# One edge product for four tiles, in both edge layers of a graph network on one core

## The reference, cut to what matters

```
def _egnn_conv(x, src, dst, edge_attr, W_msg, W_edge, W_root, b):
    msg = x[src] @ W_msg + edge_attr @ W_edge
    agg = jax.ops.segment_max(msg, dst, num_segments=x.shape[0])
    agg = jnp.where(jnp.isneginf(agg), 0.0, agg)
    return agg + x @ W_root + b
c1 = jax.nn.leaky_relu(_egnn_conv(X, src, dst, edge_attr, W1_msg, W1_edge, W1_root, b1))
c2 = jax.nn.leaky_relu(_egnn_conv(c1, src, dst, edge_attr, W2_msg, W2_edge, W2_root, b2))
x = _layernorm(x + c2)
```

## Time and profile before

| what | value |
|---|---|
| runs | 5271.81 us median of 3 (5270.69 to 5279.11) |
| profiled execution | span 5177.2 us; the page gives no other time of it |
| layer a, about 1787 to 2493 us | TensorE 449, VectorE 340, ScalarE 123, GpSimd 377 us busy in 700 |
| layer b, about 2495 to 3190 us | TensorE 351, VectorE 462, ScalarE 258, GpSimd 377 us busy in 700 |
| edge products | 782 passes in each of the two layers |

### The profile page before, as it was taken

The page is one execution under the profiler, slowest core; times in us unless marked ns, Lnnn a source line. Parts: engine busy times, 40 slices in busy tenths (PEclk is TensorE's granted clock), DMA queues, the critical chain, the costliest instruction groups (busy, mean ns, idle before and its releaser), DMA issues. The chain is left out here.

```text
span 5177.2 us, 44582 instructions
## 1 busy us (share of the span) xinstructions
PE 2118.5 (41%) x9550; PEld 1632.7 (32%) x9550; DVE 2725.0 (53%) x10673; ACT 2076.4 (40%) x4598; POOL 2694.2 (52%) x2760
## 2 busy tenths in 40 slices
PE   5111584554545556766555553677671000000000
PEld 2000241144545446655333332567671000000000
DVE  8300695655555544545466676666674343434344
ACT  9100691044444411111233333455564443544444
POOL 6677004144444355555455554555554656566564
PEclk9655895567776765666555555565565555555555
DMA  1211004833333344444354454344442222222221
GB/s 54 44 39 36 5 1 121 224 100 100 102 98 106 104 129 156 152 154 153 113 157 151 151 160 130 129 149 141 138 140 67 64 62 64 64 61 66 58 70 41
DMA packets 361464, 524.87 MB, mean 101 GB/s; under 512 B 221626, under 2 KB 230607, under 8 KB 360938
## 3 DMA queue, kind: packets, MB, share of 16 engines
q1 hardware_dynamic: 267050, 366.82, 21.4%
q0 software_dynamic: 94144, 155.21, 12.9%
HBM read 230.29 MB, written 291.54 MB: 101 GB/s over the span
## 5 line engine op out<-in xcount | busy, mean ns | idle before, releaser
L1929 POOL DMA_INDIRECT out<-O,nidx x392 | 385.9, 984 | 374.3 <-ACT O L202 255.1
L1296 POOL DMA_INDIRECT l1a_G<-t,src x391 | 378.3, 967 | 319.8 <-issue 288.4
L1615 POOL DMA_INDIRECT l_G<-t,src x391 | 385.8, 987 | 304.2 <-issue 273.2
L637 POOL DMA_INDIRECT O<-x_pad,nidx x344 | 343.2, 998 | 367.7 <-PE en_psB L836 263.3
L1296 POOL DMA_INDIRECT l1b_G<-t,src x391 | 376.3, 962 | 301.1 <-issue 277.1
L2150 PE MATMUL l_psR<-l_diag,l_ones 128*128 128x128 f32 x2 | 0.8, 502 | 1241.7 <-DVE l_diag L2004 1241.7
L967 POOL DMA_INDIRECT l_G<-xs,src x327 | 312.5, 956 | 349.8 <-DVE l_G L996 229.8
L1914 POOL DMA_INDIRECT l_G<-t,src x391 | 375.8, 961 | 168.5 <-issue 118.9
L2150 PEld LDWEIGHTS l_psR<-l_diag,l_ones 128*128 128x128 f32 x2 | 0.5, 312 | 1241.8 <-DVE l_diag L2004 1241.8
L1494 PE MATMUL l1a_psP<-l1a_w,l1a_xT 97*128 97x192 f32 x784 | 250.0, 506 | 230.5 <-ACT l1a_xT L1411 157.4
L1473 PE MATMUL l1b_psE<-l1b_we,l1b_edge 32*128 32x96 f32 x782 | 197.6, 430 | 305.1 <-DMA l1b_edge<-edge_k 220.1
(11 more groups left out here) (347 smaller groups left out, 6757.0 us busy)
## 6 DMA issues: line engine op xcount, KB each, us to landing
h<-l_G SPq DMA_DIRECT2D x96, 392.0 KB, 2.3
t<-l1b_t_out SPq DMA_DIRECT2D x48, 768.0 KB
h<-l_G SPq DMA_DIRECT2D x48, 768.0 KB
xs<-en_y SPq DMA_DIRECT2D x48, 392.0 KB
t<-l_t_out SPq DMA_DIRECT2D x48, 392.0 KB
l_H<-t SPq DMA_DIRECT2D x48, 392.0 KB
en_y<-x_pad SPq DMA_DIRECT2D x48, 384.0 KB
t<-l_tr_out SPq DMA_DIRECT2D x48, 384.0 KB
```

The lines of the kernel that those rows point to most:

```text
L637: pool.indirect_dma_start(k.O[:, at, :], None, x, bass.IndirectOffsetOnAxis(k.nidx[:, at:at + 1], 0))\
L1296: pool.indirect_dma_start(tile(c)[:, q, :], None, table, bass.IndirectOffsetOnAxis(k.src[:, at:at + 1], 0))\
L1615: pool.indirect_dma_start(tile(c)[:, q, :], None, table, bass.IndirectOffsetOnAxis(k.src[:, at:at + 1], 0))\
L1929: pool.indirect_dma_start(out, bass.IndirectOffsetOnAxis(k.nidx[:, at:at + 1], 0), k.O[:, at, :], None, bounds_check=NP - 1, oob_is_err=Fa ...
```

## The change

The edge features of four tiles are stacked on the 128 partitions (tile i on partitions 32i to 32i+31), and the weight becomes a block-diagonal matrix of 128 by 384 with four copies of the 32 by 96 weight. One product then gives four tiles at once: the 96 columns of tile i come only from the partitions of tile i, since the other blocks are zero. The chunks of two and one tile take the columns that belong to their tiles. The features are laid out accordingly by the host, each half chunk as one block of 128 rows with 128 values. VectorE clears the weight first, and SyncE waits for that and loads the weight four times into the diagonal.

```
-        we = sb("we", [DE, D])
+        we = sb("we", [PACK * DE, PACK * D])          # PACK = Q // 2 = 4
-        edge = sb("edge", [DE, 2, Q // 2 * 128])
+        edge = sb("edge", [PACK * DE, 2, 128])
+        blank = sem("blank")
...
-            sp.dma_start(we[:, :], We).then_inc(weights, 16)
+            sp.wait_ge(blank, 1)
+            for i in range(PACK):
+                sp.dma_start(we[i * DE:(i + 1) * DE, i * D:(i + 1) * D], We).then_inc(weights, 16)
...
-                    sp.dma_start(edge[:, h, :], edge_k[c][:, h * 512:(h + 1) * 512]).then_inc(edge_in[h], 16)
+                    sp.dma_start(edge[:, h, :], edge_k[c, h]).then_inc(edge_in[h], 16)
...
+            dve.memset(we[:, :], 0.0).then_inc(blank, 1)
...
-            pe.wait_ge(weights, 64 if first else 16)
+            pe.wait_ge(weights, 16 * PACK + 48 if first else 16 * PACK)
...
-                    for i in range(n):
-                        part = edge[:, at // 4, (at % 4 + i) * 128:(at % 4 + i + 1) * 128]
-                        last = pe.matmul(V(c)[:, a + i, :], part, we[:, :],
-                                         start=first, stop=True, skip_group_check=not first)
-                    last.then_inc(edged, 1)
+                    mine = we[:, at % PACK * D:(at % PACK + n) * D].rearrange("p (q d) -> p q d", q=n)
+                    pe.matmul(V(c)[:, a:a + n, :], edge[:, at // PACK, :], mine,
+                              start=first, stop=True, skip_group_check=not first).then_inc(edged, 1)
...
-    by_tile = lambda a: whole(a.reshape(128, K, DE)).reshape(128, NCH, Q, -1).transpose(1, 3, 2, 0).reshape(NCH, -1, Q * 128)
+    by_tile = lambda a: whole(a.reshape(128, K, DE)).reshape(128, NCH, 2, Q // 2 * DE).transpose(1, 2, 3, 0)
```

More of the change, by code:

```diff
@@ L1172, in layer1 @@
     HELD = 3
+    PACK = Q // 2
     ctx = ExitStack()
```

## The result

The changed kernel takes 5212.47 us (median of 6 runs, 5201.7 to 5230.79) against 5271.25 us of the kernel before (6 runs, 5244.86 to 5286.93): ratio 0.9887, 95% interval 0.9854 to 0.992. A second series gave 5215.31 against 5264.3 us, ratio 0.993 (0.9892 to 0.9967). So the gain is some 37 to 59 us where 7 were forecast.

The account below looks back on a forecast made before the run. No engine was full: TensorE's loop bound part of layer a, standstills until GpSimd's gathers ended bound the rest and layer b. Terms 0 - 7 + 0 + 0 = -7 us took 5272 to 5265 us; range 5232 to 5290.

Parts of the forecast that it names:

- What of it lies on the path: Step asking where saved edge-product time on TensorE shortens layers a and b: 7 us in a, 0 in b.
- In layer b none: Layer b: edge products end 1.0 us ahead of VectorE, nothing waits for TensorE, so the gain is 0.
- 12 x 0.6 = 7 us: Layer a: half of VectorE's 23 waits for edge products each gain 0.6 us; bounds 0 and 18 us.
- The 12 even steps: Layer a: chunks assumed to run at the pace set by TensorE's loop, 12.84 us each, gaining 0.6 us each.
- no even steps near 12.1 us: Layer a: the forecast's sign was that chunks paced by TensorE's loop would shorten from 12.84 to near 12.1 us.
- more nameless waits: Layer a, VectorE's first addition: unnamed waits, 190.0 us before, should stay about as long; more or fewer meant wrong.
- the pause: Both layers: engines begin nothing although work is ready, until GpSimd's gathers are through; GpSimd stands 7.6 us per two chunks.
- The price of a product: Edge products: half a chunk takes 1.58 us instead of 1.94 in b; a chunk saves 0.6 us in a.
- Transfers and the start of a layer: Smaller edge packets, weight clearing and four weight loads: both terms 0; uncovered, the start costs at most 4 us in all.
- Rival 4: Layer b: small packets land edge features late, lengthening about half of 49 steps; +24 us, 5296 us, chance 0.06.
- rival 5: Layer a: TensorE works less, its clock stays lower and edge products take longer; about 5276 us, chance 0.07.
- Rivals 2 and 3: Layer a: the pace set by TensorE's loop spreads, 5230 us, chance 0.17; or is lost, 5284 us, chance 0.13.

Follow-up runs that it names:

- 512 columns: Changed kernel with each edge product streaming 512 columns instead of 384, the added ones zeros; 5215.73 us, ratio 0.9929 to the kernel before.
- layout only: Changed kernel's stacked features, block-diagonal weight and loads, but again one product per tile (782 passes); 5261.98 us, ratio 1.0034 to the kernel before.
- tiny6: Changed kernel with six small extra products ahead of each edge product (1366 passes a layer); 5283.69 us, ratio 1.0079 to the kernel before.
- tiny: Changed kernel with three small extra products ahead of each edge product (782 passes a layer); 5261.31 us, ratio 1.0031 to the kernel before.

## Why the prediction failed

**The step that failed** is "What of it lies on the path": "In layer b none" and, in a, 12 x 0.6 = 7 us. Both terms price the time of TensorE and ask who waits for it. In b indeed nobody does, and 31 us of added TensorE time cost nothing (512 columns). But the change takes 584 passes of TensorE from each layer, and the number of passes has a price of its own that isn't in the sum. Pooled over the profiles:

| | 782 passes | 198 passes | difference |
|---|---|---|---|
| layer a | 706.5 (707.8, 691.1, 714.8, 712.0, 706.8) | 680.2 (694.1, 671.0, 673.1, 682.7) | -26 us |
| layer b | 711.5 (700.1, 710.6, 714.0, 715.8, 717.2) | 689.8 (688.6, 691.3, 688.1, 691.2) | -22 us |

In b the two sets don't overlap; in a they do by one profile each, 691.1 against 694.1. The terms were 7 and 0 and measured 26 and 22: 48 us by the profiles, 37 to 59 by the two timed series. On the average between these two numbers that is 45 ns a pass in a and 37 ns in b; the twice as many small products, which left b at 711.1 us, show that it isn't a fixed price.

The 12 even steps of the 7 us weren't there either. By the places where GpSimd stood for over 1.5 us, 7 of the chunks of a in before are single steps, of 11.5 to 16.4 us each, and none in after, where all chunks behind the start go in pairs. So what a gained isn't what the term counted, and of the prediction's own signs two came out against it: no even steps near 12.1 us, and more nameless waits.

**The prediction named this and gave it no chance.** Its last paragraph says that if the pause "depends on how many instructions TensorE runs, both layers move by tens of microseconds". That is what happened. It had the evidence for a mechanism that doesn't go by waits on TensorE: 190 us of nameless waits in a, 4.59 us of idleness ahead of an instruction that needed only its own engine's results. A mechanism that takes 6 to 7 us out of every 27 deserved to be a rival with a price, even a rough one. That ScalarE's instructions count as well was not seen.

How the number acts shows in b. In before, VectorE is often held up well ahead of the last gathers too. Of before, the timeline of VectorE:

```profile
2824.53 1.92 DVE L1355 SCALAR_TENSOR_TENSOR l1b_R<-l1b_G,lastok,l1b_R 128x96 f32<-128x96 f32 x8
2828.26 0.97 DVE L1365 SCALAR_TENSOR_TENSOR l1b_psL<-l1b_R 128x768 f32<-128x768 f32 x1 [1.80 <-issue]
2829.67 0.95 DVE L1367 TENSOR_TENSOR O<-O,l1b_psL 128x768 f32<-128x768 f32 x1 [0.45 <-issue]
```

Line 1365 needs only VectorE's own results; its idle time in all was given above, 30.9 to 58.5 us with 782 passes and 4.3 to 9.0 with 198. GpSimd's mean idle time at the end of a pair in b, beyond the usual 0.30 us, is 6.3 to 7.1 us in the five kernels with 782 passes, 5.9 to 6.1 in the four with 198 and 7.1 with the ScalarE instructions. The means of the first two groups, 6.7 and 6.0, differ by 0.7 us; over 22 pairs that is 15 of the 22 us.

**The price of a product** was set too high. Half a chunk was to take 1.58 us in b; it takes 1.44 from 2809.81 to 2811.25 and 1.28 from 2812.53 to 2813.81, at a granted clock of 0.50 as in the earlier trace rows. So half a chunk saves 0.5 to 0.66 us at that level, not 0.36. In a, at the higher level, the four passes take 1.30 us from start to start (2074.96 to 2076.26), where 1.45 to 1.58 were expected. In b nothing waited for the difference. The rule weighed there (the Trainium skill, "TensorE: Matmul & The Clock Gate", Part 2, time set by the columns) would have forecast no gain, as the sum of time in b did. Its 0 fails for the same reason: neither counts the instructions.

**Transfers and the start of a layer** cost nothing that can be seen: 1.0034 (0.9998 to 1.0071) for both together (layout only), and 0.9887 with them in. Rival 4 is out.

**The clock** went the other way than rival 5 feared. In b it is 0.50 in each kernel with 32-row edge products and 0.59 to 0.65 in each with 128-row ones, with 198, 782 or 1366 passes. The Trainium skill ("TensorE: Matmul & The Clock Gate", Part 1) says that the gate goes by how busy TensorE has been. In b busy time fell from 351 to 247 us and the clock rose, so busy time as the profile counts it doesn't tell it. By layout only it is worth no time here; in the stretch of after shown above it is 0.50 while the edge products run, as it was before.

**Rivals 2 and 3**, the even pace spreading or lost, aren't what moved b, which has no single step in any profile but that of tiny6, with three. In a the even pace comes and goes with one and the same kernel: 7 single steps in before, 32 in its repeated run, which took 691.1 us where the others with 782 passes took 707 to 715. That makes it a part of the scatter in a; the kernels with 198 passes had 0 to 5 such steps and took 671 to 694 us.

**The calibration** was wrong as well. The 94.6 us between span and median were put outside the span. The profiled execution of after took 5218.63 us with a span of 5216.9: 1.7 us lie outside. So the profiled execution of before took about 5179 us, less than any timed run of it; the three timed runs, 5270.69 to 5279.11, had shown too little of the spread. The sum of differences isn't touched by it. The bound of 0.2% for what can be told is: 0.35% is nearer.

**What stays open.** Which shared thing holds the instructions up isn't shown. It isn't the TensorE clock or the DMA packets (layout only), and it isn't TensorE's time. A rival that no run tried is the fetching of the instructions themselves, of which the change needs less. The DMA queues that do it, over 2495 to 3190 us, first in before and then in after:

```profile
q14 instruction: 31, 0.25, 0.1%
q8 instruction: 8, 0.13, 0.1%
...
q14 instruction: 30, 0.25, 0.1%
q8 instruction: 4, 0.07, 0.0%
```

Over the whole span queue 8 has its packets by the number of TensorE's passes (78 in before, layout only and tiny, 69 in after, 87 in tiny6), and queue 14 goes from 192 to 205 with the ScalarE instructions. But in b 8 or 4 packets of queue 8 stand against more than 20 pauses, so it isn't one fetch of TensorE's for each pause; more the counts don't tell. One other possible cause is the profiler's own record path. The Trainium skill ("NOTIFIC — the notification-queue block", section "Overflow: three behaviours, one of which stalls the engine") says that the block which writes the trace records holds back its producers when its internal queues are full. No run here shows it. All runs here have the profiler's span and clock, so whether the slowness exists without the profiler wasn't tried.

## What to carry to other kernels

Where waits end that the profile can't name, and engines that wait for nothing stand still together, count instructions as well as busy time: here, averaged over one step in their number each, a TensorE pass cost 37 to 45 ns and a short ScalarE instruction 36 to 39 ns of the layer, though ScalarE was idle over 440 of 700 us and TensorE over 250. Where GpSimd gathers far ahead, try to hold it nearer to its consumer; one tighter wait gave about as much as the whole change. And read a gain of 1% from stage lengths pooled over several profiles that share the property, not from one pair of them.

## What the runs showed of the hardware

- Late in a long run of indirect gathers, and some 2.5 us beyond it, instructions of ScalarE and VectorE can get slow to start: one-column ScalarE instructions 0.1 us apart otherwise came 0.7 to 1.4 us apart, and VectorE's chain of eight took 6 us instead of 3.04. Not all were: eight of VectorE ran in 1.38 us in the middle of it, and the gathers kept their 1.25 us.
- The layer takes longer with more instructions, on TensorE or ScalarE: 584 passes fewer per layer gave 26 and 22 us, 832 short ScalarE instructions more cost 30 and 32 us. VectorE's idle time ahead of an instruction that waits for neither went from 4.3 to 9.0 us up to 30.9 to 58.5 and 56.9. It isn't proportional: with 1366 passes b took 711.1 us, with 782 a mean of 711.5.
- In b a float32 product of 128 rows by 384 columns took 1.28 us and four of 32 rows by 96 took 1.94, both at a granted clock of 0.50.
- The granted clock of TensorE in b was 0.50 with products of 32 rows and 0.62 with as many products of 128 rows.
